# A selective scan's C products: sixteen of 128 per call move from VectorE to GpSimd

## What is computed

```
dA  = exp(dt[..., None] * A)
dBx = dt[..., None] * B[:, :, None, :] * x[..., None]
def step(h, inp):
    h = dA_t * h + dBx_t
    y = einsum('bdn,bn->bd', h, C_t)       # sum over the 16 states n
y = scan(step) + D * x
```

## Time and profile before

| | us |
|---|---|
| median of 3 runs | 3865.53 (3864.57 to 3865.61) |
| profiled execution, its own time | 3856.49 |
| its span in the profile | 3854.8 |
| first scan call (layer 0), first to last scan starts | 1120.5 to 1286.6 |
| second and third scan call (layer 1), first to last scan starts | 3350.7 to 3723.5 |

### The profile page before, as it was taken

The page is one execution under the profiler, slowest core; times in us unless marked ns, Lnnn a source line. Parts: engine busy times, 40 slices in busy tenths (PEclk is TensorE's granted clock), DMA queues, the critical chain, the costliest instruction groups (busy, mean ns, idle before and its releaser), DMA issues. The chain is left out here.

```text
span 3854.8 us, 75904 instructions
## 1 busy us (share of the span) xinstructions
PE 3619.2 (94%) x32856; PEld 2526.8 (66%) x32856; DVE 2254.2 (58%) x2469; ACT 1607.5 (42%) x2213; POOL 1281.2 (33%) x792
## 2 busy tenths in 40 slices
PE   7999999999779779999999999999999998797998
PEld 4555556555345555788888888888888846454554
DVE  4666666666369852555555555555555515697972
ACT  2555555555269421222222222222222103697950
POOL 4344344342048520222222222222221004285861
PEclk8999999999789889999999999999999999898999
DMA  6455555553111032111111111111111112111110
GB/s 209 126 136 148 141 140 147 141 138 103 41 55 52 12 142 80 29 42 41 49 41 49 41 41 50 41 49 41 49 41 45 72 42 55 41 51 31 52 45 22
DMA packets 215252, 277.14 MB, mean 72 GB/s; under 512 B 67056, under 2 KB 165328, under 8 KB 213632
## 3 DMA queue, kind: packets, MB, share of 16 engines
q1 hardware_dynamic: 214920, 272.28, 24.3%
HBM read 218.63 MB, written 53.13 MB: 70 GB/s over the span
## 5 line engine op out<-in xcount | busy, mean ns | idle before, releaser
L1727 POOL TENSOR_TENSOR D_ctx_lo<-D_ctx_raw,D_ctx_hi 128x2048 fp32r<-128x2048 f32 (+1 forms) x64 | 269.7, 4214 | 1217.8 <-ACT D_ctx_hi L1721 1217.8
L724 DVE TENSOR_REDUCE A_mxc<-A_psX 128x2 f32<-128x768 f32 (+2 forms) x512 | 485.4, 984 | 206.1 <-PE A_psX L754 205.2
L1020 ACT ACTIVATE A_probs<-A_psE 128x1024 f32<-128x1024 f32 (+1 forms) x416 | 426.3, 1025 | 317.3 <-PE A_psE L1053 312.0
L1746 ACT ACTIVATE D_V<-D_psY 128x384 f32<-128x384 f32 x208 | 101.9, 490 | 904.3 <-PE D_psY L1812 904.3
L1762 DVE TENSOR_REDUCE D_mxc<-D_psE 128x4 f32<-128x1536 f32 (+2 forms) x128 | 241.9, 1890 | 235.0 <-PE D_psE L1840 235.0
L2103 ACT ACTIVATE D_probs<-D_psE 128x2048 f32<-128x2048 f32 x112 | 210.4, 1879 | 295.6 <-PE D_psE L2216 295.6
L330 POOL TENSOR_TENSOR ES_hcp<-E_du,E_Cn 128x512 f32<-128x512 f32 x224 | 284.8, 1275 | 128.3 <-DVE E_du L357 97.9
L2232 PE MATMUL D_psO<-D_probs,D_V 128*32 128x256 f32 (+1 forms) x5376 | 313.4, 381 | 0.0
L1802 PE MATMUL D_psY<-D_ctx_hi,D_wk_hi 128*128 128x384 f32 (+2 forms) x768 | 279.9, 364 | 13.4 <-DVE D_K_lo L1757 12.7
L1812 PE MATMUL D_psY<-D_wv_hi,D_ctx_hi 128*128 128x384 f32 x832 | 285.3, 343 | 0.0
L1812 PE MATMUL D_psY<-D_wv_hi,D_ctx_lo 128*128 128x384 f32 x832 | 279.0, 335 | 0.0
(11 more groups left out here) (369 smaller groups left out, 7793.9 us busy)
## 6 DMA issues: line engine op xcount, KB each, us to landing
A_land<-in_ctx SPq DMA_DIRECT2D x32, 768.0 KB, 6.1
D_ctx_raw<-in_ctx SPq DMA_DIRECT2D x32, 768.0 KB, 4.7
A_land<-in_ctx SPq DMA_DIRECT2D x16, 1024.0 KB, 5.7
D_ctx_raw<-in_ctx SPq DMA_DIRECT2D x16, 1024.0 KB, 5.4
E_Cn<-bc_scratch SPq DMA_DIRECT2D x64, 256.0 KB, 3.3
k_scratch<-A_Khl SPq DMA_DIRECT2D x32, 384.0 KB, 5.2
A_Kst<-k_scratch SPq DMA_DIRECT2D x64, 192.0 KB, 3.6
A_land<-in_ctx SPq DMA_DIRECT2D x16, 642.0 KB, 4.4
```

The source lines that it names most:

```text
L724: nc.vector.tensor_reduce(mxc[:, u % 4, :, u // 4], psX[:, x % 2, :, 0:w], axis=AX_X, op=ALU.max).then_inc(x_free, 1)
L1020: nc.scalar.activation(probs[0:KW[k], n % NPR, :, :].rearrange("p h q -> p (h q)"), psE[0:KW[k], :], ACT.Exp, scale=HD ** -0.5).then_inc(e ...
L1727: nc.gpsimd.tensor_tensor(ctx_lo[c][:, :, 0:w], ctx_raw[c][:, :, 0:w], ctx_hi[c][:, :, 0:w].bitcast(F32), ALU.subtract).then_inc(lo_done[c ...
```

## The change

`c_on_pool` returns True for every step.

```
 def c_on_pool(half, n, c):
-    return c > 0 or n % 2 == 1
+    return True
```

## The result

The changed kernel takes 3871.26 us (median of 9 runs, 3867.67 to 3879.75) against 3865.11 for the kernel before in the same group of runs: +6.15 us, ratio 1.0022 with a 95% interval of 1.0014 to 1.0031. Run again in a second group it took 3871.54 against 3862.12, ratio 1.0032 (1.0020 to 1.0045). For this repetition +6 to +8 us had been expected; it is +9.4. The forecast was 3871.6, a rise of 6.1, under the 7.7 us that it took for the least that can be told from none. Both intervals lie above 1, so the change is slower, by 0.2 to 0.3%.

The account below looks back on a forecast made before the run. TensorE was taken to bound the scan calls, with a thin lead. L0 0.34 and each L1 call 2.9 us total 6.1; 3865.5 + 6.1 = 3871.6 us, no measurable difference, range 3865.5 to 3877.0.

Parts of the forecast that it names:

- VectorE's 32 us worth nothing, GpSimd's 61 us hidden in plain steps: Plain scan steps: 48 products leave VectorE without direct gain; on GpSimd, TensorE hides them, 9.92 us against 10.37 per eight.
- The rival that its pitch is its duration: L1 second halves: GpSimd's gapless pitch is 1.275 us, not 1.24; 9.8 us slower in all, 3875.3; chance 0.25.
- The ring gets tight, 0.85 us of slack: Scan output and product buffers: all four turn every four steps, so GpSimd may be 0.85 us late before TensorE stalls.
- Gates, 0.33 + 3 x 0.55 = 2.0 us per L1 call: L1 second halves: GpSimd's four gated outputs stall TensorE 0.33 us at the first, 0.55 at each later one.
- The cover of the rival: Gates of L1 calls: VectorE's freed time or ring slack hides the stalls; +0.5 us in all, 3866.0; chance 0.12.
- Between the halves, 0: VectorE's four finishes between the halves: the existing 0.84 us stall per call stays unchanged; bounds -0.84 and +0.5.
- Tail, 0.24 in the L0 call, 0.8 in an L1 call: Call ends: GpSimd's last product delays the L0 call's last add 0.24 us and VectorE's first gate 0.8 per L1 call.
- Head, 0.1 us per call: Call starts: the first add moves behind step 7's transposes, 1.32 us of work in 1.22; 0.1 us per call.
- The clock rival: Call heads: the moved first add alters TensorE's clock falls, 1.5 us each; -1.5 or +3.0, 3870.1 to 3874.6; chance 0.10.

Follow-up runs that it names:

- 3: The changed kernel with six buffers in place of four for the scan's SBUF output and the product; +3.3 us to the kernel before, ratio 1.0009.
- 5: The changed kernel without GpSimd's four gated outputs in each L1 call; +4.8 us to the kernel before, ratio 1.0018.
- 6: The changed kernel, first add still late, with TensorE's pauses in turns 0 to 4 filled with 32 unused transposes; +4.2 us to the kernel before, ratio 1.0012.
- experiment 2: The kernel before with the add of step 0 in turn 4 instead of 2, its product still on VectorE; +3.6 us to the kernel before, ratio 1.0012.
- experiment 4: The changed kernel with six buffers and the add of step 0 back in turn 2; -2.3 us to the kernel before, ratio 0.9992.

## Why the prediction was right, and where it was not

- *VectorE's 32 us worth nothing, GpSimd's 61 us hidden in plain steps:* right. Adds stay 1.30 us apart, VectorE waits for GpSimd's products as foretold, and GpSimd's pitch alone is 1.236, so TensorE is still the bound. The rival that its pitch is its duration falls.
- *The ring gets tight, 0.85 us of slack:* right, shown from both sides by 3 (more buffers) and 5 (no gates).
- *Gates, 0.33 + 3 x 0.55 = 2.0 us per L1 call:* 2.00 (1.72 behind the gates and 0.28 after the second) and 1.85 measured. The cover of the rival did not appear.
- *Between the halves, 0:* nearly; +0.35, +0.06 and +0.06, within the bounds.
- *Tail, 0.24 in the L0 call, 0.8 in an L1 call:* right; 0.25, and 0.65 at VectorE's first gate.
- *Head, 0.1 us per call:* this is the step that failed. It counted the work behind the turn at full clock. The moved add takes TensorE's work out of the first microseconds, and the clock falls in calls 1 and 3 and stays low in call 2: 2.0, 0.2 and 2.6 us. The clock rival named the mechanism, at 0.10, and its price of 1.5 a fall was low; it should have been a term of the sum, since the kernel before already showed one such fall.

So the steps sum to 6.1, the calls grew by 10.7 in the profile, of which the heads are the 4.5 that were missing. The medians say +6.2 and +9.4: that the forecast met the first within 0.1 us is luck, as its sum left out its largest term. Why the medians grew by less than the profiled calls is not shown; the quick profiled execution of the kernel before may be part of it. Open too is why the clock falls in call 2 even with the early add. That filled pauses keep it up there is shown by 6; why, in the kernels with the early add, it rises sooner in call 2 than in call 1 is not.

## To carry to other kernels

When one engine bounds a loop with a few per cent to spare, moving work to the next engine is free only as long as the buffers between them hold its worst lateness, so work the ring through at the places where extra work comes in (here the gates and the step between the halves); two more buffers took all stalls away here. Look at the order on TensorE at the start of a stage as well: an add that comes two turns later can cost more than the forty-eight products that were moved (+3.6 us in experiment 2, without any move). Where TensorE starts a stage in pieces, read the granted clock in windows of a few microseconds, and fill the pauses.

## What the runs showed of the hardware

A GpSimd product's recorded duration (1275 ns) is longer than its pitch without a gap, 1.236 us over twelve in a row. TensorE's granted clock was at 0.50 to 0.57 from 8 to 12 us after the first scan in 15 of 15 heads with the late add, and at 1.00 in all six with the pauses filled, at the price of 32 transposes without a use. Where the clock was low in that window, turn 7 came 1.5 us (call 3 of experiment 4, 13.4) to 3.0 us (call 3 of experiments 2 and 3, 14.9) later than the 11.9 of a head at 1.00.
